# Second attention: VectorE's part of the square in one piece, placed ahead of the second absolute value

## The reference

```python
S = jnp.einsum('bhnd,bhmd->bhnm', Q, K) / dh ** 0.5
W_tau = jax.nn.softmax(S, axis=-1)
W_sigma = 1.0 / ((1.0 + jnp.abs(S) / b_) ** 2 + t_ ** 2)
W_sigma = W_sigma / W_sigma.sum(axis=-1, keepdims=True)
tau = jnp.einsum('bhnm,bhmd->bhnd', W_tau, V)
sigma = jnp.einsum('bhnm,bhmd->bhnd', W_sigma, V)
f = 0.5 * tau + 0.5 * sigma
```

## Time and profile before

| What | us |
|---|---|
| Median of 3 runs (lowest to highest) | 2975.97 (2975.95 to 2976.5) |
| The profiled execution, its own time | 2972.06 |
| Its span, first to last instruction | 2970.4 |
| GpSimd's first shift to its last product's start in the second attention | 1224.77 to 2684.0 |

### The profile page before, as it was taken

One profiled execution on the slowest core, in us unless ns is written; L12 is line 12 of the kernel. 1 busy time (PEld: TensorE's weight loads), 2 busy tenths in 40 slices (PEclk: granted clock), 3 DMA queues, 4 the chain that ended last, 5 costly groups with the idle time before them and its releaser, 6 DMA issues. The chain is left out here.

```text
span 2970.4 us, 60006 instructions
## 1 busy us (share of the span) xinstructions
PE 2445.4 (82%) x18487; PEld 1018.8 (34%) x18614; DVE 2491.1 (84%) x3983; ACT 2234.4 (75%) x2441; POOL 1992.1 (67%) x1236
## 2 busy tenths in 40 slices
PE   3755999998577994689999999999999999983898
PEld 2642333333474662122222222222222222222566
DVE  4666888885577657799999999999999999996765
ACT  4532777777364543499999999999999999993554
POOL 4510222222453651499999999999999999994465
PEclk9976999999687997699999999999999999997799
DMA  3222111000120002000000000000000000000000
GB/s 116 70 64 87 30 29 29 28 27 11 45 79 5 1 0 86 22 15 14 16 15 14 14 16 15 14 14 16 15 14 14 16 15 14 14 5 0 1 12 18
DMA packets 93504, 76.58 MB, mean 26 GB/s; under 512 B 32480, under 2 KB 73960, under 8 KB 93264
## 3 DMA queue, kind: packets, MB, share of 16 engines
q1 hardware_dynamic: 89104, 66.36, 7.8%
q0 software_dynamic: 4288, 8.82, 0.9%
HBM read 47.77 MB, written 24.42 MB: 24 GB/s over the span
## 5 line engine op out<-in xcount | busy, mean ns | idle before, releaser
L1761 POOL TENSOR_TENSOR a_sg<-a_sg,all_f0w 128x1632 f32<-128x1632 f32 x256 | 940.7, 3675 | 21.3
L1967 DVE TENSOR_REDUCE a_mx<-a_pm 128x1 f32<-128x1024 f32 x512 | 618.3, 1208 | 23.2 <-PE a_pm L1813 23.2
L1978 DVE TENSOR_SCALAR a_sg<-a_pa 128x1024 int32<-128x1024 int32 x512 | 614.9, 1201 | 3.8 <-PE a_pa L1813 3.8
L1894 ACT ACTIVATE a_pt<-a_pb 128x1024 f32<-128x1024 f32 x512 | 532.4, 1040 | 55.0 <-PE a_pb L1813 53.4
L1831 PE MATMUL a_po<-a_pt,a_Vh 128*32 128x512 f32 x2048 | 538.4, 604 | 15.0 <-ACT a_osb L1913 11.4
L1831 PE MATMUL a_po<-a_sg,a_Vh 128*32 128x512 f32 x2048 | 538.3, 604 | 0.0
L1758 POOL TENSOR_SCALAR all_f0w<-a_sg,a_parh 128x1632 f32<-128x1632 f32 x256 | 506.7, 1979 | 37.4 <-DVE a_sg L1978 37.3
L1903 ACT ACTIVATE a_sg<-a_sg,a_parh 128x2048 f32<-128x2048 f32 x256 | 517.0, 2020 | 0.0
L1907 ACT ACTIVATE a_sg<-a_sg 128x2048 f32<-128x2048 f32 x256 | 496.0, 1937 | 0.0
L1581 ACT ACTIVATE a_pt<-a_ring 128x1024 f32<-128x1024 f32 (+2 forms) x384 | 313.7, 846 | 164.4 <-PE a_ring L1508 161.2
L1653 DVE TENSOR_REDUCE a_mx<-a_ring 128x2 f32<-128x1024 f32 (+3 forms) x384 | 359.2, 955 | 85.1 <-PE a_ring L1491 66.1
(11 more groups left out here) (265 smaller groups left out, 4457.9 us busy)
## 6 DMA issues: line engine op xcount, KB each, us to landing
all_Q<-q_parts SPq DMA_DIRECT2D x256, 48.0 KB
all_K<-k_parts SPq DMA_DIRECT2D x256, 48.0 KB
k_parts<-p_parts SPq DMA_DIRECT2D x16, 384.0 KB, 2.6
e_recs<-routed_rows SPq DMA_DIRECT2D x70, 64.5 KB, 1.9
n_xn<-expert_rows SPq DMA_DIRECT2D x16, 256.0 KB, 4.2
all_Q<-a_rows SPq DMA_DIRECT2D x256, 2.0 KB
q_parts<-p_parts SPq DMA_DIRECT2D x16, 192.0 KB, 2.3
q_parts<-p_parts SPq DMA_DIRECT2D x8, 384.0 KB, 2.6
```

The costliest lines, as they stand in the source:

```text
L1761: nc.gpsimd.tensor_tensor(buf[:, :, 0:CUT], buf[:, :, 0:CUT], sums, ALU.mult)\
L1894: nc.scalar.activation(pt[(j - LT) % 4][:, i, :], pb[:], ACT.Exp, scale=SC)\
L1967: nc.vector.tensor_reduce(mx[:, (j // PER) % 2, t:t + 1], pm[:], AX.X, ALU.max)\
L1978: nc.vector.tensor_scalar(sg[(j - LS) % 4][:, i, :].bitcast(I32), pa[:].bitcast(I32), SIGN_OFF, None, ALU.bitwise_and).then_inc(abs_done, 1)
```

## The change

`CUT` now counts from the start of the slot's buffer: VectorE's part is the first 13 x 1024 / 32 = 416 elements of tile 0, and GpSimd's is the rest of tile 0 and all of tile 1, 1632 elements in one piece. The scratch buffers are cut to the same size in one piece. VectorE's instruction moves from the end of the step to the place between the maximum of tile 1 (and the small `output` work there) and the absolute value of tile 1, and it waits for the first absolute value only. GpSimd still waits for both.

```diff
@@ -1675,7 +1675,7 @@
     UNROLL = PER * RING
     LS, LT, LE, LP = 5, 7, 7, 8
     SC = DH ** -0.5
-    CUT = 51 * T // 64
+    CUT = 13 * T // 32
     WIDE = TT * (DH + 1)
     with ExitStack() as ctx:
         m = Mem(nc, ctx, tag)
@@ -1686,8 +1686,8 @@
         rows = m.sb("rows", [TT, MAX_PARTS, P], BF16)
         pt = [m.sb(f"pt{r}", [P, 2, T]) for r in range(4)]
         sg = [m.sb(f"sg{r}", [P, 2, T]) for r in range(4)]
-        shifted = [scratch[:, 4 * CUT * r:4 * CUT * (r + 1)].bitcast(F32).rearrange("p (i n) -> p i n", i=2)
-                   for r in range(2)]
+        REST = 2 * T - CUT
+        shifted = [scratch[:, 2 * REST * r:2 * REST * (r + 1)].bitcast(F32) for r in range(2)]
         osb = m.sb("osb", [P, CH])
         rz = m.sb("rz", [P, 4, 4])
         fw = m.sb("fw", [P, 4, 4, DH])
@@ -1747,7 +1747,8 @@
                     s = at(it, j, LS)
                     if s is None:
                         return
-                    buf, sums = sg[(j - LS) % 4], shifted[(j - LS) % 2]
+                    buf = sg[(j - LS) % 4][:].rearrange("p i n -> p (i n)")[:, CUT:]
+                    sums = shifted[(j - LS) % 2]
                     if some(s, 2):
                         pool.wait_ge(sq_pool, s - 1)
                     if (j - LS) % PER == 0:
@@ -1755,10 +1756,10 @@
                     pool.wait_ge(abs_done, 2 * s + 2)
                     pool.nop(nofuse=True)
                     b2 = parh[:, ring(j, LS), 0:1]
-                    nc.gpsimd.tensor_scalar(sums, buf[:, :, 0:CUT], b2, 1.0, ALU.add, ALU.mult)\
+                    nc.gpsimd.tensor_scalar(sums, buf, b2, 1.0, ALU.add, ALU.mult)\
                         .then_inc(shift_done, 1)
                     pool.wait_ge(shift_done, s + 1)
-                    nc.gpsimd.tensor_tensor(buf[:, :, 0:CUT], buf[:, :, 0:CUT], sums, ALU.mult)\
+                    nc.gpsimd.tensor_tensor(buf, buf, sums, ALU.mult)\
                         .then_inc(sq_pool, 1)
 
                 slots(pool, body)
@@ -1971,20 +1972,19 @@
                             output(it, j, 0, LP + 3)
                         else:
                             output(it, j, 1, LP + 3)
+                        if i == 1 and ss is not None:
+                            share = sg[(j - LS) % 4][:, 0, 0:CUT]
+                            dve.wait_ge(abs_done, 2 * ss + 1)
+                            if (j - LS) % PER == 0:
+                                dve.wait_ge(head_in[ring(j, LS)], HEAD_LOADS * rounds(it, j, LS))
+                            nc.vector.scalar_tensor_tensor(share, share, parh[:, ring(j, LS), 0:1], share,
+                                                           ALU.add, ALU.mult).then_inc(sq_dve, 1)
                         if ss is not None:
                             dve.wait_ge(abs_mm, 2 * ss + i + 1)
                             if some(ss, 4):
                                 dve.wait_ge(pv_done, 2 * (ss - 4) + i + 1)
                             nc.vector.tensor_scalar(sg[(j - LS) % 4][:, i, :].bitcast(I32), pa[:].bitcast(I32),
                                                     SIGN_OFF, None, ALU.bitwise_and).then_inc(abs_done, 1)
-                    if ss is not None:
-                        buf = sg[(j - LS) % 4]
-                        dve.wait_ge(abs_done, 2 * ss + 2)
-                        if (j - LS) % PER == 0:
-                            dve.wait_ge(head_in[ring(j, LS)], HEAD_LOADS * rounds(it, j, LS))
-                        nc.vector.scalar_tensor_tensor(buf[:, :, CUT:T], buf[:, :, CUT:T],
-                                                       parh[:, ring(j, LS), 0:1], buf[:, :, CUT:T],
-                                                       ALU.add, ALU.mult).then_inc(sq_dve, 1)
                     negated(it, j, 0, 1)
                     output(it, j, 2, LP + 3)
 
```

## The result

The changed kernel takes 3335.28 us (median, 3334.1 to 3335.8, 6 runs) beside 2975.84 us for the kernel before (6 runs): ratio 1.121, 95% interval 1.1196 to 1.1225. The profiled execution took 3335.8 us, its span 3334.1.

The account below looks back on a forecast made before the run. GpSimd was taken to bound the second attention at 5.71 us per slot. Turn-taking makes it 7.04: 255 slots x 1.33 = +339 us, first slot +0.1, on 2972.06 gives 3311, plus 3.9 for the median 3315 us; range 3275 to 3400.

Parts of the forecast that it names:

- the side to which 0.92 had been given: Whole kernel: the change makes it slower, chance 0.92, against 0.06 for within 0.2% and 0.02 for faster.
- GpSimd binds before, and VectorE's fullness is waiting: Second attention before the change: GpSimd sets 5.71 us per slot; VectorE's 99% busy includes waiting inside the square.
- The square makes no progress while the product runs: Second attention: VectorE's square, 0.65 us undisturbed, is stuck during GpSimd's product and ends 0.46 us after it.
- The rival that the square isn't locked out: Second attention: the square runs through GpSimd's product at 0.65 us, time stays 2976 us; chance 0.02.
- Taking turns, and that each slot hands it on: Second attention: abs 1 waits behind the square, GpSimd for abs 1; 1.33 us more in each of 255 slots.
- The terms of the slot: Second attention, from one product's end to the next: seven times summing to 7.04 us per slot against 5.71.
- shift alone: GpSimd's shift without the square in it: 1.52 us instead of 1.97; if it gains nothing, +115 us.
- The 3.9 us that the forecast added for the median: Whole kernel: median of timed runs over the profiled execution, taking 3311 to 3315 us.
- The bounds of the shape: Second attention: one piece instead of two costs nothing, within -0.05 to +0.05 us per slot, +-13 us in all.
- The square beside the shift: Second attention: a square ready before GpSimd's product begins would run beside the shift, as before the change.
- VectorE a slot ahead, as a state that carries itself: Second attention: with the next square ready before the product, slots stay 5.71 us, time 2976 us; chance 0.05.
- TensorE's clock: Second attention: TensorE, 73% busy, drops to half clock and binds, 3450 to 3800 us, 4150 at worst; chance 0.04.

Follow-up runs that it names:

- e1: Changed kernel with only the new division of the work kept, the square back at the end of the step: 2974.5 us, ratio 0.9997 to the kernel before.
- e5: Changed kernel with GpSimd waiting in every slot for one absolute value more before its shift: 3212.94 us, ratio 1.0798 to the kernel before.
- e9: Changed kernel with GpSimd's product cut into two instructions of 816 elements: 3005.86 us, ratio 1.0101 to the kernel before.
- e2b: Changed kernel with the square's first operand read from PSUM and its second operation a maximum, output differing from the reference: 2955.99 us, ratio 0.9943.
- e3: Changed kernel with GpSimd waiting for one absolute value more before the very first shift only: 3334.27 us, ratio 1.1209 to the kernel before.

## Why the prediction was right, and where it wasn't

The forecast was 3315 us, the result 3335, in the range and on the side to which 0.92 had been given. Its steps:

- *GpSimd binds before, and VectorE's fullness is waiting.* Right. With the square no longer shut out (one input in PSUM) it is 0.64 us and ScalarE takes over, busy in 1300.00 of 1300 us; the estimate for this from ScalarE's 5.66 us gave 2950 to 2976, and 2956 came.
- *The square makes no progress while the product runs.* Right, at every length: behind the first slot the changed kernel's squares last 0.86 to 4.05 us, and all 255 end 0.45 us after a product's end. The rival that the square isn't locked out falls by the same numbers.
- *Taking turns, and that each slot hands it on.* Right. It broke only where the square had an input in PSUM, where the shift was held back in every slot, or where the product was cut.
- *The terms of the slot.* Expected, then the mean of 255 slots of the changed kernel: square's end after the product 0.46, 0.450; overlap with the absolute value -0.07, -0.077; absolute value 1.20, 1.211; release 0.17, 0.173; shift alone 1.52, 1.625; gap 0.08, 0.083; product 3.68, 3.664; slot 7.04, 7.129. **The mis-sized term is the shift**: 0.105 us, 255 x 0.105 = 27 us, more than the whole miss of 20. (Between the profiled executions the miss is 25 us, 3311 to 3335.8: 255 x 0.089 = 23 in the slots, the rest outside them. The 3.9 us that the forecast added for the median had no counterpart in the result.) Two readings had agreed on 1.52 and both were off. The line through the copies gave 1517 ns for 1632 elements, but a shift, which adds and multiplies, takes 1625. The other reading took off 0.46 us, the time until the square ends; what the shift had lost to it was 1.97 - 1.62 = 0.35. The other 0.12 us until the square's end cost the shift nothing, and the same difference shows in other places (last section).
- *The bounds of the shape.* Zero was taken and zero came (e1).
- *The square beside the shift* (in the rival of a slot ahead). Wrong in its wording, without a price here: the square runs between two instructions of GpSimd, also at the shift. That is why e5 and e9 work.
- *VectorE a slot ahead, as a state that carries itself.* The rival didn't come, and its argument has a hole. It said that 1.6 us of delay decide and that VectorE's sum of 5.2 us keeps it. 3.2 us of delay gave two slots, at the lower clock. The sum of one engine doesn't tell whether a lead lasts; the way back through ScalarE and TensorE counts, and so do other instructions of the locked kind (the sum of 64 elements).
- *TensorE's clock.* It fell a little: 0.93 over the stage where it had been 1.00, TensorE 78% busy. VectorE's idle time before its maxima, which wait for TensorE, rose from 23 to 74 us in all, but that comes out of the square's waiting, and by the products' starts in the trace nine slots in ten took 7.10 to 7.16 us; the 118 in which the granted clock was 1.00 throughout and the 137 others both took 7.13 us in the mean. It cost nothing that can be seen, so this rival is rejected, though its sign (a clock below 1.00) appeared.

## What to carry to other kernels

Before an instruction is moved up in VectorE's queue, look whether it is of the kind that GpSimd shuts out (here: two SBUF inputs, or a `tensor_scalar` from SBUF to SBUF), and what comes behind it: where VectorE is shut out until a GpSimd instruction ends, everything queued behind is shut out too, and if GpSimd waits for any of it, the two take turns. A duration that varies for the same shape (here 0.75 to 1.14 us) and always ends at the same distance from another engine's event is a wait inside an instruction, and a busy share hides it. Three things took the turn-taking away here: an operand in PSUM (e2b, in a kernel that computes something else), nothing behind the instruction for which the other engine waits soon (the kernel before), and GpSimd's long instruction in pieces (e9, which still takes 30 us more than the kernel before).

## What the runs showed of the hardware

- The granularity is one GpSimd instruction: squares that came while a shift was at work waited for its end as those in a product did, and a square that came 0.03 us after a product's start waited all of its 3.67 us (4.09 us in all). A GpSimd instruction that VectorE holds up lets a second VectorE instruction, directly behind the first, go ahead too (L1956, 62 times).
- It doesn't hold for every GpSimd instruction. In the feed-forward block with experts of the kernel before, VectorE's L430 and L432, with two SBUF inputs, begin 11 times under a `DMA_INDIRECT` of GpSimd and take 0.16 to 0.19 us, as without one.
- The price to GpSimd is the time from its instruction's start to the end of VectorE's, less some 0.12 to 0.15 us. In the means of the traces: 0.47 us to the square's end and 0.35 paid (256 shifts before), 0.36 and 0.22 (250 products in e5), 0.49 and 0.34 (250 second halves in e9); in the output stage 1.05 and 0.90 (L1217 behind L1264).
- It isn't a matter of size: 64 elements lasted 2.57 us.
- A single-tensor `tensor_scalar` from SBUF to SBUF is shut out as well, and needs half the time once it is let in (0.24 against 0.45 us until its end); BATCH_NORM_STATS2 with one SBUF input isn't (0.28 us under a product and without).
- After a square had come 0.03 us behind a product's start, the turn-taking, at 1.6 us more per slot than the slots ahead of it, was there for the 253 slots that followed (e3). That an arrival those hundredths earlier would have kept the lead isn't shown.
